# Scans over one block of channels each, with one weighing between every two of them, in a Mamba/MoE plus linear-attention kernel

## The reference, cut to what matters

```python
def step(carry, inp):
    dA_t, dBu_t, C_t = inp
    carry = dA_t * carry + dBu_t
    y_t = jnp.einsum('bdn,bn->bd', carry, C_t)
    return (carry, y_t)
# deltaA = exp(dt * A),  dBu = dt * B * x,  A = -exp(A_log)
y = ys.transpose(1, 0, 2) + x * D
return y * _silu(z.transpose(0, 2, 1))
```

## Time and profile before

| | us |
|---|---|
| median of 3 runs | 3095.49 |
| profiled execution | 3098.88 |
| its span | 3097.0 |
| VectorE busy, whole span | 2255.7 (73%) |
| TensorE busy, whole span | 2569.9 (83%) |
| one batch of the first layer (838.0 to 1080.2 us) | 242.2 |
| VectorE busy in it | 228.4 |
| GpSimd busy in it | 206.2 |
| TensorE busy in it | 195.5 |
| ScalarE busy in it | 187.8 |

### The profile page before, as it was taken

The page is one execution under the profiler, slowest core; times in us unless marked ns, Lnnn a source line. Parts: engine busy times, 40 slices in busy tenths (PEclk is TensorE's granted clock), DMA queues, the critical chain, the costliest instruction groups (busy, mean ns, idle before and its releaser), DMA issues. The chain is left out here.

```text
span 3097.0 us, 36581 instructions
## 1 busy us (share of the span) xinstructions
PE 2569.9 (83%) x13286; PEld 1693.4 (55%) x13286; DVE 2255.7 (73%) x2797; ACT 1777.0 (57%) x2734; POOL 1733.8 (56%) x567
## 2 busy tenths in 40 slices
PE   5457788788788798788787787678999999999999
PEld 2233655655565565565565565555555556455554
DVE  8689899899999999999999999964244243342430
ACT  4456587688687677777867867522232232332322
POOL 2899788788888879879978978831010010110000
PEclk9668899899899899899999999887999999999999
DMA  7222343334333324333333333341010010110000
GB/s 267 73 74 68 113 142 110 109 122 141 114 120 116 131 97 148 111 110 116 131 125 122 113 116 129 116 152 42 1 34 24 10 34 0 34 34 0 7 7 7
DMA packets 143590, 272.65 MB, mean 88 GB/s; under 512 B 23031, under 2 KB 94174, under 8 KB 142430
## 3 DMA queue, kind: packets, MB, share of 16 engines
q1 hardware_dynamic: 137310, 254.12, 24.2%
q0 software_dynamic: 6144, 16.79, 1.6%
HBM read 230.75 MB, written 40.11 MB: 87 GB/s over the span
## 5 line engine op out<-in xcount | busy, mean ns | idle before, releaser
L1037 POOL TENSOR_TENSOR hs<-u,bb 128x2048 f32<-128x2048 f32 x256 | 1159.2, 4534 | 237.7 <-PE hT L1255 231.7
L1167 DVE TENSOR_TENSOR_SCAN hs<-dA,hs 128x1024 f32<-128x1024 f32 x512 | 1162.7, 2277 | 88.2 <-POOL hs L1037 45.5
L1255 PE MATMUL hT<-ident,hs 128*128 128x128 f32 x3648 | 576.2, 299 | 358.4 <-DVE held L1179 307.5
L1083 ACT ACTIVATE dA<-dt,cols 128x511 f32<-128x511 f32 x1024 | 661.0, 680 | 299.3 <-DVE hs L1167 294.2
L1255 PEld LDWEIGHTS hT<-ident,hs 128*128 128x128 f32 x3648 | 441.9, 152 | 512.8 <-DVE held L1179 207.0
L1179 DVE SCALAR_TENSOR_TENSOR held<-hT,ct,held 128x512 f32<-128x512 f32 x880 | 609.7, 733 | 26.5 <-PE hT L1255 26.0
L1526 ACT ACTIVATE gl<-bank,cols_sb 128x512 f32<-128x512 f32 x192 | 130.6, 687 | 527.4 <-PE bank L1765 527.2
L1765 PE MATMUL bank<-mT,cms_sb 128*128 128x512 f32 x768 | 362.7, 597 | 10.1 <-ACT mT L1520 8.6
L144 POOL COPY cur<-slot 128x8 uint32 (+1 forms) x8 | 1.5, 188 | 640.1 <-DVE held L156 628.4
L1274 PEld LDWEIGHTS moe<-xgT,held 128*128 128x128 f32 x2272 | 293.0, 207 | 53.7 <-issue 27.7
L1274 PE MATMUL moe<-xgT,held 128*128 128x128 f32 x2272 | 306.2, 292 | 12.3 <-ACT xgT L1098 12.0
(11 more groups left out here) (228 smaller groups left out, 3248.7 us busy)
## 6 DMA issues: line engine op xcount, KB each, us to landing
held<-wl SPq DMA_DIRECT2D x71, 1024.0 KB
bb<-b_scratch SPq DMA_DIRECT2D x128, 512.0 KB, 5.1
held<-wl SPq DMA_DIRECT2D x71, 512.0 KB
xg<-xg_scratch SPq DMA_DIRECT2D x71, 128.0 KB
yg_scratch<-yg SPq DMA_DIRECT2D x71, 128.0 KB, 1.7
held<-x SPq DMA_DIRECT2D x16, 512.0 KB, 6.4
xg_scratch<-zero SPq DMA_DIRECT2D x8, 1024.0 KB, 6.8
cb<-b_scratch SPq DMA_DIRECT2D x28, 256.0 KB, 5.8
```

The lines of the kernel that those rows point to most:

```text
L1037: nc.gpsimd.tensor_tensor(hs[n % HS][:, :, :], u[d][:, :, :], row, ALU.mult).then_inc(dBu_ready, 1)
L1083: last = nc.scalar.activation(dst, src, ACT.Exp, scale=cols[:, at:at + 1])
L1167: nc.vector.tensor_tensor_scan(h, decay, h, 0.0, ALU.mult, ALU.add).then_inc(scan_done, 1)
L1255: last = nc.tensor.transpose(hT[c % 2][:, k * P:(k + 1) * P], hs[n % HS][:, k, c * P:(c + 1) * P], ident[:, :])
```

## The change

Three things change together.

The scan of 1024 positions over two blocks becomes two scans of 512 over one block each. `dA` becomes four tiles of one block, each with a semaphore count of its own, where it was two tiles of two blocks. ACT waits and signals per block. The counts that others wait for go from two to four per state.

In each half step VectorE issues a scan of one block, then `finish` and `gate` where they stand, one weighing, the scan of the other block, and the other weighing.

The tables are other ones: pieces move by one to fifteen half steps, `LATE` has 12 entries for the forward unit where it had 7, the last tile of a unit starts one half step later, the skip is added two steps later, and the weighing of the second half of state 1 in a forward unit moves from half step 4 to 5.

```diff
-        BEHIND, TURNED = (1, 2, 3, 4), (0, 1, 2, 3)
+        BEHIND, TURNED = (1, 2, 3, 5), (0, 1, 2, 3)
...
-        plan(0, "dt", (14, 16, 18, 20))
+        plan(0, "dt", (15, 16, 17, 21))
...
-        TILE_AT = ((0, 6, 12, 19, 25), (0, 6, 12, 19, 25))
+        TILE_AT = ((0, 6, 12, 19, 26), (0, 6, 12, 19, 26))
...
-            dA = [ps(f"dA{j}", [P, HF, L], lay0) for j in range(2)]
+            dA = [ps(f"dA{k}", [P, L], lay0) for k in range(DB)]
...
-                    act.wait_ge(scan_done, 2 * step + j + 1)
                     for k in range(HF * j, HF * j + HF):
+                        act.wait_ge(scan_done, DB * step + k + 1)
                         at = AL + (d * DB + k) * NS + n
...
-                        last = nc.scalar.activation(dst, src, ACT.Exp, scale=cols[:, at:at + 1])
-                    last.then_inc(dA_ready, 1)
+                        src = dt[d][:, k, 1:] if d == 0 else dt[d][:, k, :][:, ::-1][:, 1:]
+                        nc.scalar.activation(dA[k][:, 1:], src, ACT.Exp, scale=cols[:, at:at + 1]).then_inc(dA_ready, 1)
...
-                    dve.wait_ge(dA_ready, 2 * step + j + 1)
-                    if j == 0:
+                    dve.wait_ge(dA_ready, DB * step + k + 1)
+                    if k == 0:
                         dve.wait_ge(dBu_ready, step + 1)
-                    h = hs[n % HS][:, HF * j:HF * j + HF, :].rearrange("p k l -> p (k l)")
-                    decay = dA[j][:, :, :].rearrange("p k l -> p (k l)")
+                    h = hs[n % HS][:, k, :]
                     if d == 1:
                         h = h[:, ::-1]
-                    nc.vector.tensor_tensor_scan(h, decay, h, 0.0, ALU.mult, ALU.add).then_inc(scan_done, 1)
+                    nc.vector.tensor_tensor_scan(h, dA[k][:, :], h, 0.0, ALU.mult, ALU.add).then_inc(scan_done, 1)
...
+                                ahead(d, unit, n + 2, 2 * j, more)
...
-                                for m, c in blocks[2 * n + j]:
+                                some = blocks[2 * n + j]
+                                for m, c in some[:1]:
                                     weigh(d, unit, m, c)
+                                ahead(d, unit, n + 2, 2 * j + 1, more)
+                                for m, c in some[1:]:
+                                    weigh(d, unit, m, c)
```

More of the change, by code:

```diff
@@ L277, in bass_mamba_moe_then_linear_attention_mlp @@
         plan(0, "xd", (12,))
-        plan(0, "dt", (14, 16, 18, 20))
+        plan(0, "dt", (15, 16, 17, 21))
         plan(0, "soft", (21,))
-        plan(0, "c", (16,))
-        plan(1, "gate", (20, 21, 22, 24))
+        plan(0, "c", (31,))
+        plan(1, "gate", (20, 22, 24, 25))
         plan(1, "conv", (4, 6, 7, 8))
-        plan(1, "silu", (8,))
+        plan(1, "silu", (9,))
         plan(1, "xd", (10,))
         plan(1, "dt", (11, 12, 13, 15))
-        plan(1, "soft", (16,))
-        plan(1, "c", (17,))
+        plan(1, "soft", (17,))
+        plan(1, "c", (18,))
         OUT = {0: 0, 2: 1}
@@ L1000, in weigh @@
                     m = POOLN[k]
-                    pool.wait_ge(scan_done, 2 * (NS * unit + m) + 4)
+                    pool.wait_ge(scan_done, DB * (NS * unit + m) + 2 * DB)
                     pool.wait_ge(cb_in, 16 * (NP * (unit - 2) + k + 1))
@@ L1192, in gate, with ahead @@
                     last.then_inc(hE_ready, 1)
+                def ahead(d, unit, n, k, more):
+                    if n < NS:
+                        scan(d, unit, n, k)
+                    elif more:
+                        scan(1 - d, unit + 1, n - NS, k)
                 def finish(b, k):
@@ L1204, in body @@
                             for j in range(2):
-                                if n + 2 < NS:
-                                    scan(d, unit, n + 2, j)
-                                elif more:
-                                    scan(1 - d, unit + 1, n + 2 - NS, j)
+                                ahead(d, unit, n + 2, 2 * j, more)
                                 for k in range(DB) if d == 0 and later(b) else ():
@@ L1214, in body @@
                                         gate(b, i)
-                                for m, c in blocks[2 * n + j]:
+                                some = blocks[2 * n + j]
[3 more added lines that the diff above has]
+                                for m, c in some[1:]:
                                     weigh(d, unit, m, c)
                 for n in range(2):
-                    for j in range(2):
-                        scan(0, 0, n, j)
+                    for k in range(DB):
+                        scan(0, 0, n, k)
                 batches(dve, body)
@@ L1251, in turn @@
                     if c == 0:
-                        pe.wait_ge(scan_done, 2 * (NS * unit + n) + 4)
+                        pe.wait_ge(scan_done, DB * (NS * unit + n) + 2 * DB)
                     pe.wait_ge(hT_used, 4 * turned(unit, n) + c + 1)
```

18 lines of the change are left out of this document (7 added, 11 removed).

## The result

The changed kernel takes 3191.31 us (median; 3190.44 to 3192.54), the kernel before 3095.19 beside it: ratio 1.0305 (1.0293 to 1.0317). That is 96 us slower, where 19 were predicted and 53 were the end of the range. The first layer's part of the trace holds all of it.

A forecast was written before the change was run, and what follows sets the result against it. VectorE's own work was taken to bound the first layer (94% busy per batch). Scans +32, ScalarE -37, TensorE +29 and batch end -5 gave +19 us: 3118 profiled, 3114 median; 8-in-10 range 3074 to 3148.

The forecast's parts named there:

- The scans: VectorE: 512 more, shorter scans cost 66 ns each, some hidden by waits: +32 us, bounds 0 and 73.
- The full fixed price: Third rival, VectorE: short scans overlap less, each costing up to 143 ns; sum +60, 3155 us; chance 0.12.
- ScalarE's side: Finer decays give ScalarE room, so VectorE waits 5.3 us less per batch: -37 us, bounds 0 and -42.5.
- The arithmetic of rows 6: Two VectorE waits for ScalarE, 1.29 and 2.33 us per batch, both go as four decays move ahead of dt.
- the prediction's own test: If VectorE's waits for ScalarE stay above 20 us, the arithmetic of rows 6 is wrong.
- TensorE's side: Room for TensorE's pieces before first weighings falls from 4.7 to 3.7 us: +29 us, bounds 0 and 67.
- The named places: Four heavy places per batch where TensorE is late, each to cost 1.07 us more: 30 us over 7 batches.
- The end of a batch: down and transposes of C fill TensorE's gap before the first sum: -5 us, bounds -10 to +10.
- The same scans between it and the last weighings: At a batch's end, finish keeps two half scans between it and the last weighings; part of the -5 us.
- faster by about as much: The first sum, late by what fills the gap, gains about as much or more at full rate: -0.7 us per batch.
- The held clock: First rival: evenly spaced turns keep TensorE's clock at 2.4 GHz, so it is not late more often; -24, 3072 us; chance 0.28.
- Cancelled terms: Second rival: TensorE's loss is a third of that counted, as one wait gives room at the next; 0, 3095 us; chance 0.15.

The follow-up runs named there:

- the weighings together: The form alone with both scans of a half step before both weighings: 3106.29 us, 1.0031; same edit in the changed kernel, new tables: 3094.94 us, 0.9997.
- The form alone: The changed kernel with every table as before (scans of one block, a weighing between every two): 3154.34 us, 1.0192 to the kernel before.
- The tables alone: The kernel before (scans of two blocks, weighings in pairs) with the new tables: 3102.00 us, 1.0027.
- the heavy half steps: The form alone, weighings apart only in 22 half steps behind 2.6 us or more of TensorE's pieces and a forward unit's first: 3141.56 us, 1.0141.
- less work on TensorE: The changed kernel with half of the expert products left out (half the contraction in a and b, two of four down blocks): 3124.28 us, 1.0090.
- the last tile and the C piece: The changed kernel with the last tile's start back to half step 25 and the C piece back to 16: 3193.62 us, 1.0314.
- raised to 0.961: The form alone with every turn in half steps without pieces done three times on TensorE: 3180.70 us, 1.0273.
- the 34 light half steps: The form alone, weighings apart only where TensorE's pieces of the half step before are under 2.6 us, together elsewhere: 3118.95 us, 1.0067.

## Why the prediction was wrong, step by step

**The scans: right.** +32 us predicted, +29 found, 57 ns each where 66 were taken. In the runs this term is bought back: with the weighings together, waits shrink so far that the kernel is only 10 us slower. The full fixed price (143 ns, the third rival) is ruled out. With it falls, for this pair of instructions, the rule of the Trainium skill (VectorE: DVE Perf Modes, section The DRAIN you can't avoid) that the next operation waits for the empty pipe; the same page's section Two Vector instructions with no wait between them lets an instruction start earlier when its operands start in the same group of partitions as those before, and the 1.13 us from a scan of 1.21 to the weighing agree with that.

**ScalarE's side: the place right, the sum not.** -37 predicted, -14 found. The arithmetic of rows 6 held: 2.33 and 1.29 are 0 after, and 1.48 of the earlier trace rows is 0.32. What was left out is that the decays of half step 17 stand behind pieces that wait for TensorE: in the forward unit because 17 is new in `LATE`, in the backward one because a `dt` piece moved in ahead of them. They cost 1.11 us in forward half step 19 and 2.96 in the backward one. The form alone has neither. The tables alone have 2.97 in the forward one and nothing in the backward one, and with the weighings together it is 0.88 and 0.83: the backward one needs both, the moved piece and a TensorE that is late. By the prediction's own test (over 20 us left, so the arithmetic is wrong) one would have drawn the wrong conclusion from the 28.2.

**TensorE's side: the step that failed.** The mechanism was named rightly, 3.7 us of room for the pieces in place of 4.7, and the runs bear it out: the weighings together undo the whole loss, the heavy half steps hold 35 of the form's 48 us, and less work on TensorE returns 67 of 96. The term was sized at +29 and measured +57 ahead of weighings and +19 ahead of gates. Three things in it were wrong.

First, it multiplied by the wrong places. It took places that were late already and added 1.07 us to each. The waits of each place per batch, mean of four batches:

| place | before | together | form alone | after | predicted change |
|---|---|---|---|---|---|
| forward 25, weighing | 0.58 | 0.47 | 0.73 | 2.43 | +1.07 |
| backward 2, weighing | 2.63 | 0.26 | 2.71 | 2.39 | +1.07 |
| forward 11 and 12, weighing | 0 | 0 | 0.33 | 0.88 | +1.07 |
| forward 2, first state's weighing | 1.16 | 1.06 | 1.06 | 1.06 | +1.07 |
| forward 4 and 23, gate | 0.48 | 1.04 | 1.86 | 3.19 | none |
| forward 31 and backward 0, weighing | 0 | 0 | 1.78 | 2.21 | none |
| forward 28 and backward 25, weighing | 0.36 | 0 | 1.25 | 1.73 | none |

The named places rose by 2.4 us per batch, not 4.3; those not named rose by 6.3. Most of them had been just in time, and a wait that is not there has no row. Ahead of the first weighing of a pair VectorE waited 37 times in the stage before and 95 times after, about 1.0 us each time in both.

Second, it kept TensorE's pace at a place fixed. The place of the earlier trace rows seems not to have moved, but two shifts cancel there. Before, the weighing starts 5.90 us after the projection (967.25 to 973.15) and VectorE was free after 3.28. In the changed kernel it starts after 4.24, because the projection now runs at the full clock, and VectorE was free after 1.84. So the room did shrink, by 1.4 us, and the clock gave 1.7 back. With the weighings together the projection runs at the full clock too and VectorE is free after 3.98: against that kernel the room shrank by 2.1 us. That the clock would rise just there was luck, and no sum had it.

Third, it stopped at the weighing. Gate, `finish` and ScalarE's late decays wait for the same engine. Whatever reads a piece is late with it.

**The tables: not weighed at all as a term.** They cost 5 us in the old form, gain 11 with short scans in pairs, and cost 37 with the weighings apart. The prediction used them for ScalarE's gain, and had them relieve one place of TensorE; that they move work about on an engine with less room was in none of its sums. Which entries cost the 37 us isn't shown: the last tile and the C piece, taken back, returned nothing.

**The end of a batch: wrong.** -5 predicted, +14 found. "The same scans between it and the last weighings" read the order of VectorE and not the wait of TensorE. In the earlier trace rows the first sum waits until the last pair of weighings is over. Of the scans behind that pair, a whole half step's stood before `finish`; now the last weighing stands behind the second scan, and only one scan of 1.13 us lies between. `finish` waits 4.25 us per batch, 2.24 before. That `down` and the transposes of C fill TensorE's gap there is not the cause: taken back, they leave 4.51, since the sum then runs at the lower clock, as the prediction's "faster by about as much" has it. With all old tables it is 2.80 as a mean: 2.04 in batches where the sum runs at a granted clock of 1.00, 3.41 and 3.70 in others. Why the clock is up there in some batches stays open.

**The rivals.** The held clock did not come about: the mean fell from 0.924 to 0.906, and where it was raised to 0.961, by work of its own, nothing was gained. At the one place of the earlier trace rows it did rise, as that rival had it. Cancelled terms: the case exists, but for another order, that of the weighings together. Why the 34 light half steps cost 13 us is settled in part: half of the waits they add stand at the heavy half step of the earlier trace rows, so lateness is handed on, and the clock there takes part in it. How it is handed on, and whether each turn's own wait and restart costs anything, no run here tells.

## What to carry to other kernels

When an order on the busiest engine is made more even, ask what the uneven order gave the engine behind it: two consumers side by side leave one long gap for the producer, the same two spread out leave two short ones, and a producer that works in order with two buffers needs the long one. Work out that gap before and after, and hold it against every piece that the producer does there, those that are just in time above all, because the places that will be late are mostly not the ones that are late now. Compare one place in two kernels only after a look at the rate at which its pieces ran: a wait that stays the same can be room lost and clock gained. A table of slots belongs to its order: the same table gave -11, +5 and +37 us in three orders, so tune and judge it only in the form in which it runs.

## What the hardware showed that was not expected

The extra cost of a short scan was 57 ns between weighings (2255.7 to 2285.0 us busy for 512 more scans), close to the 66 read from one row before. With two scans in a row it was 47 ns (2255.7 to 2279.6): they start 1.12 us apart (x2 in 2.33 us, where one takes 1.21).

Between kernels TensorE's mean granted clock said nothing of the time here. It was 0.924 in the kernel before, 0.961 in one 85 us slower, 0.883 in one 67 us faster than the changed kernel at 0.906, and 0.924 with the weighings together and the new tables, which took the time of the kernel before. Between executions of one kernel it goes with the time: the tables alone took 3096.71 us at 0.926 and 3119.25 at 0.915. Which of the two follows the other isn't shown.

Work that fills an engine's gap can cost nothing. At the end of a batch `down` and the transposes of C delay the first sum by 2.3 us, but it then runs at a granted clock of 1.00 where it is 0.50 without them, and `finish` waits no longer (4.25 us per batch, 4.51 without).
